# Splitting two pieces of the query weights before the key pieces are taken, and squaring the values after the first query piece's scaling

## The reference

```python
q = x @ Wq + x @ q_A @ q_B          # 16 heads of 64
k = x @ Wk + x @ k_A @ k_B          # 4 heads
v = x @ Wv + x @ v_A @ v_B          # 4 heads
q = _rms_norm(q); k = _rms_norm(k)
q = _apply_rope(q, cos, sin); k = _apply_rope(k, cos, sin)
q = q * q_gain
...                                 # causal softmax attention, y
norm = jnp.sqrt(jnp.sum(v_bt * v_bt, axis=-1, keepdims=True))
vn = v_bt / jnp.maximum(norm, 1e-12)
proj = jnp.sum(y_g * vn, axis=-1, keepdims=True) * vn
out = (y_g - proj) @ Wproj + (y_g - proj) @ p_A @ p_B
```

## Time and profile before

| | before |
|---|---|
| time, three executions | 1453.94, 1456.71, 1459.86 us; median 1456.71 us |
| the profiled execution | 1463.41 us, its span 1461.8 us |
| PE busy | 1416.0 us, 97% of the span |
| DVE, ACT, POOL busy | 844.9 us (58%), 529.3 us (36%), 203.7 us (14%) |
| mean granted clock of TensorE | 0.988 of full speed |

### The profile page before, as it was taken

The page is one execution under the profiler, slowest core; times in us unless marked ns, Lnnn a source line. Parts: engine busy times, 40 slices in busy tenths (PEclk is TensorE's granted clock), DMA queues, the critical chain, the costliest instruction groups (busy, mean ns, idle before and its releaser), DMA issues. The chain is left out here.

```text
span 1461.8 us, 18196 instructions
## 1 busy us (share of the span) xinstructions
PE 1416.0 (97%) x6676; PEld 1156.6 (79%) x6676; DVE 844.9 (58%) x1232; ACT 529.3 (36%) x947; POOL 203.7 (14%) x264
## 2 busy tenths in 40 slices
PE   7999999999999999999999999799998999998998
PEld 6888788888888888888888888676777888877786
DVE  5564455555454545555454556578765576765655
ACT  3222322322233222322223212565432436665561
POOL 3000100000000000000000000555211022122132
PEclk9999999999999999999999999999999899999999
DMA  7353643333333333333333322201100566876766
GB/s 255 144 201 116 264 161 112 116 108 114 130 109 114 108 123 121 115 108 109 134 108 114 110 94 87 87 1 59 34 1 1 179 224 234 287 270 213 269 224 216
DMA packets 43486, 203.64 MB, mean 139 GB/s; under 512 B 5232, under 2 KB 5296, under 8 KB 31984
## 3 DMA queue, kind: packets, MB, share of 16 engines
q1 hardware_dynamic: 30016, 152.32, 29.8%
q0 software_dynamic: 9568, 36.35, 7.8%
q10 hardware_dynamic: 3840, 14.16, 2.4%
HBM read 182.36 MB, written 20.45 MB: 139 GB/s over the span
## 5 line engine op out<-in xcount | busy, mean ns | idle before, releaser
L32 PE MATMUL banks<-V_hi,b_PT_hi 128*128 128x512 f32 x512 | 205.6, 401 | 0.0
L32 PE MATMUL banks<-K_hi,QT_hi 128*128 128x512 f32 x512 | 199.9, 390 | 2.5 <-PEq L157 2.5
L34 PE MATMUL banks<-V_hi,b_PT_lo 128*128 128x512 f32 x512 | 200.2, 391 | 0.0
L1024 ACT ACTIVATE b_PT_hi<-banks 128x512 fp32r<-128x512 f32 x64 | 38.4, 599 | 446.5 <-PE banks L757 446.5
L34 PE MATMUL banks<-K_hi,QT_lo 128*128 128x512 f32 x512 | 200.0, 391 | 0.0
L33 PE MATMUL banks<-K_lo,QT_hi 128*128 128x512 f32 x512 | 199.9, 390 | 0.0
L33 PE MATMUL banks<-V_lo,b_PT_hi 128*128 128x512 f32 x512 | 199.6, 390 | 0.0
L1249 DVE TENSOR_TENSOR b_scores<-banks,b_scores 128x512 f32<-128x512 f32 x64 | 44.2, 691 | 203.4 <-PE banks L34 203.4
L642 POOL DMA_DIRECT2D b_scores<-mask x60 | 32.3, 539 | 640.8 <-PE banks L757 622.9
L2183 DVE TENSOR_TENSOR e_lo<-e_raw,e_hi 128x1024 fp32r<-128x1024 f32 x80 | 94.8, 1230 | 42.0 <-ACT e_hi L2019 40.9
L32 PEld LDWEIGHTS banks<-K_hi,QT_hi 128*128 128x128 f32 x512 | 96.5, 189 | 22.9 <-issue 2.9
(11 more groups left out here) (327 smaller groups left out, 2764.9 us busy)
## 6 DMA issues: line engine op xcount, KB each, us to landing
raw<-kv SPq DMA_DIRECT2D x60, 1024.0 KB, 4.7
e_raw<-w_up SPq DMA_DIRECT2D x40, 512.0 KB, 5.3
e_raw<-w_down SPq DMA_DIRECT2D x40, 512.0 KB, 6.1
b_scores<-mask POOLq DMA_DIRECT2D x64, 256.0 KB, 2.9
d_s_raw<-shared_w SPq DMA_DIRECT2D x32, 512.0 KB, 5.0
raw<-xattn_w SPq DMA_DIRECT2D x11, 1024.0 KB, 4.8
y_dram<-c_zeros ACTq DMA_DIRECT2D x1, 6656.0 KB, 28.1
raw<-attn_w SPq DMA_DIRECT2D x6, 1024.0 KB, 4.7
```

The costliest lines, as they stand in the source:

```text
L32: pe.matmul(out, lhs_hi, rhs_hi, start=first, stop=False)
L34: return pe.matmul(out, lhs_lo, rhs_hi, start=False, stop=last)
L1024: act.activation(PT_hi[:, u % 2, :], T_ps[:, u % 2, :], ACT.Copy).then_inc(b["pt_hi"], 1)
```

## The change

ACT now rounds weights w = 3 ahead of the copy of the low rank products, w = 4 right behind that copy and ahead of take_piece(0), and w = 5 behind take_piece(0) instead of behind take_piece(3). DVE takes the remainder of w = 3 ahead of `lr_s`, and those of w = 4 and w = 5 ahead of the first turn_by_cos. The values' squares stand behind turn_by_cos(4) instead of ahead of it. PE's, POOL's and SP's programs are as they were, and no operation is added or removed. The new file is seven lines shorter, so a line of DVE's part has a number lower by 2 in it up to L1437, and by 1 or more behind it.

```diff
                 weights_hi(2)
+                weights_hi(3)
                 act.wait_ge(s["lr_ready"], 1)
                 act.wait_ge(b["pv_ready"], STEPS)
                 act.activation(lr_hi[:, :], bank[:, 6, :], ACT.Copy).then_inc(s["lr_hi"], 1)
-                weights_hi(3)
+                weights_hi(4)
                 take_piece(0)
-                take_piece(1)
-                weights_hi(4)
-                take_piece(2)
-                take_piece(3)
                 weights_hi(5)
-                take_piece(4)
+                for i in range(1, 5):
+                    take_piece(i)
                 take_piece(5)
...
                 dve.tensor_scalar(gain[:, :], gain[:, :], float(HD) ** -0.5, None, ALU.mult).then_inc(s["gained"], 1)
+                weights_lo(3)
                 dve.wait_ge(s["lr_hi"], 1)
                 dve.wait_ge(b["y_cleared"], 16)
                 dve.scalar_tensor_tensor(lr_s[:, :], f32(lr_hi[:, :]), stack_mask[:, 0:1], bank[:, 6, :],
                                          ALU.mult, ALU.add).then_inc(s["lr_lo"], 1)
                 dve.tensor_tensor(lr_lo[:, :], bank[:, 6, :], f32(lr_hi[:, :]), ALU.subtract).then_inc(s["lr_lo"], 1)
-                weights_lo(3)
                 dve.wait_ge(s["gained"], 1)
+                weights_lo(4)
+                weights_lo(5)
                 turn_by_cos(0)
-                turn_by_cos(1)
-                rotate(0)
-                weights_lo(4)
-                turn_by_cos(2)
-                rotate(1)
-                turn_by_cos(3)
-                rotate(2)
-                weights_lo(5)
-                rotate(3)
+                for i in range(1, 5):
+                    turn_by_cos(i)
+                    rotate(i - 1)
                 unit_values()
-                turn_by_cos(4)
                 rotate(4)
```

## The result

The changed kernel takes 1452.46 us (median of 20 runs, 1449.02 to 1456.09), the kernel before 1457.40 (20 runs): a ratio of 0.9966, interval 0.9956 to 0.9977, which is 4.9 us less (3.4 to 6.4). The forecast was 6.2 less, 1450.5 for a median of 1456.7, with a range of 1446 to 1454.5.

A forecast was written before the change was run, and what follows sets the result against it. TensorE, busy 97%, bounds the kernel. Waits of 2.81 and 4.53, slow clock 2.1 and restarts 0.5 put it 10.0 us ahead; the chain leaves 7.8, then 6.2: 1456.7 - 6.2 = 1450.5 us, range 1446 to 1454.5.

The forecast's parts named there:

- the five cases: Whole kernel: 1449.0 to 1452.0 (0.48), 1447 (0.28), 1452.5 (0.14), 1451.9 (0.06), slower, up to 1464 (0.04).
- the third rival: PE's new waits from 938 to 951 us cost clock: one slow stretch, about 2 us, giving 1452.5; chance 0.14.
- The splits are in time: Remainders come before PE wants them, w = 4 by 2.3 us and w = 5 by 1.65; w = 3 costs nothing.
- The chain up to root(4): POOL, held until DVE's remainder ends at 924.6, goes through roots and sines without pause; root(4) ends at 934.25.
- From root(4) to the last rotation: DVE after 934.25: sums done at 938.95, rotation of piece 4 at 939.7; PE's turn_piece(4) waits 1.7 us.
- Granted clock 1.00 from 925 to 938: Sign expected in the changed profile: full clock in that stretch, around PE's piece 5 and first turnings.
- with the longer one the slow clock behind it: PE's piece 5: removing the 4.53 us wait also removes the slow clock behind it, worth 2.1 us.
- a fall between 938 and 960 us: Sign that the prediction is wrong: the granted clock falls in this stretch, from the last turnings into the heads.
- The sum: Whole kernel: 6.2 us kept at step 2's transposes; 1463.4 becomes 1457.2, or 1450.5 from the median 1456.7.
- POOL's power and root(5): Together 4.9 us, from 939.0 to 944.0; DVE waits for that root in step 0, cutting 7.8 us to 6.2.
- The sums' move is worth 0: DVE: moving the values' squares gives 0, being ahead of the last rotation and POOL's power either way.
- The rival that took the rule literally for the power: POOL's power holds DVE's rotation of piece 4, leaving 4.8 us, so 1451.9; chance 0.06.

The follow-up runs named there:

- e6: Changed kernel with w = 5 back at its old place (copy behind take_piece(3), remainder behind rotate(2)), w = 3 and w = 4 still early; ratio to before 1.0003.
- e3: Changed kernel with 10 discarded matmuls ahead of turn_piece(4) and 3 behind it, filling PE's waits; ratio to before 1.0003.
- e10: Changed kernel with 8 discarded matmuls ahead of turn_piece(4) and none behind it; ratio to before 0.9983.
- e0: The changed kernel run again, nothing altered, as the measure for runs beside it; ratio to before 0.9973.
- e5: Changed kernel with only POOL's order changed: root(5) ahead of the power of the values' sums; ratio to before 0.9976.
- e1: Changed kernel with the values' squares and sums put back ahead of turn_by_cos(4); ratio to before 0.9974.
- e2: Kernel before with only turn_by_cos(4) moved ahead of rotate(3) and the values' squares and sums; ratio to before 1.0000.
- e4: Changed kernel with the values' sums behind the last rotation on DVE, and root(5) ahead of the sums' power on POOL; ratio to before 0.9956.
- e7: Changed kernel with rotate(3) ahead of turn_by_cos(4) instead of behind it; ratio to before 0.9975.
- e4_again: The e4 kernel run again, as the measure for e9 on the same chip; ratio to before 0.9946.
- e9: e4 with POOL's power of the values' sums behind root(6) and DVE's values' unit rows in step 2 behind turn_by_cos(6); ratio to before 0.9955.

## Why the prediction was right, and where its steps were off

- **The number.** 1452.46 us lies in the range, but four of the five cases put their times there, so that says little. It lies outside the forecast's own 1449.0 to 1452.0 and at the third rival's 1452.5, to which the prediction gave 0.14. The gain came from the cause that was named; how much of it would be kept was taken too high, 6.2 for 4.9 us.
- **The splits are in time**: right in each place. The load of w = 3 landed as computed, the copies of w = 4 and w = 5 began within 0.1 us of the forecast behind the four products, and turn_piece(0) came 10.0 us ahead. e6 shows that all of it hangs on w = 5.
- **The chain up to root(4)**: right to 0.2 us, with POOL held by the remainder.
- **From root(4) to the last rotation**: this is the term that was mis-sized. The step read "the scaling and cosines of piece 4 take 1.6 us, a rotation 0.7 to 0.8", from rows in which no sine had begun ahead of them; behind sines they took 1.6 us longer, of which 0.2 was made good by the chain ahead, and the last rotation ended at 24.28 instead of 22.97. I had counted POOL held by DVE, and not DVE held by POOL. The wait was 2.42 us instead of 1.7. The trace before had shown it: a key piece's scaling takes 0.42 us with no sine beside it and 0.67 behind one, in the very stretch of which the prediction noted only that POOL's rows had their plain length. Rows of DVE, DVE and POOL, before:

```profile
920.50 0.42 DVE L1304 TENSOR_TENSOR c_key_piece<-c_key_piece,c_ms 128x256 f32<-128x256 f32 x1 [4.29 <-POOL c_ms L654]
...
929.86 0.67 DVE L1304 TENSOR_TENSOR c_key_piece<-c_key_piece,c_ms 128x256 f32<-128x256 f32 x1 [0.56 <-POOL c_ms L654]
...
929.80 1.05 POOL L663 TENSOR_TENSOR c_sq<-c_key_piece,c_sin 128x128 f32<-128x128 f32 x2
```

- **"Granted clock 1.00 from 925 to 938"**: right, and not enough. The step "with the longer one the slow clock behind it" goes took 2.1 us of gain as kept. The clock fell again behind the new wait. That was the third rival, and it is what happened. The prediction had named a fall between 938 and 960 us as a sign that it was wrong, and this sign came.
- **The sum.** The forecast had step 2 at 34.1 behind the four products; it came at 36.4. e3 and e10, with full clock there, have it at 35.4. So of the 2.3 us missing, 0.9 are the clock; the 1.4 left over fit the 1.3 by which the last rotation was late, which is a subtraction and was not run by itself. It then carried through: 3.9 us at step 2, 3.9 (e0) at SP's load of the shared weights, 4.9 (3.4 to 6.4) and 3.9 (2.3 to 5.7) in the two measured times.
- **POOL's power and root(5)**: sized rightly (5.0 us from the sums), but they were not the limit, as e5 shows: behind the slow clock PE was late as well, and DVE waited 1.28 us for the second scores. With the clock full, in e3, DVE waits 1.60 us for that root; whether it is the limit there was not run.
- **The sums' move is worth 0**: right by e1 and e2. What I passed over is that the sums stood in the chain on either side of turn_by_cos(4): behind the last rotation (e4) they are out of it.
- **The skill's rule.** The Trainium skill (SBUF — State Buffer, SBUF: two separate sides) has whichever of the two starts first hold the port pair for its whole instruction. Here the sines at 934.13 held rotate(3), 1.83 us instead of 0.75, which agrees. POOL's powers hold no product of DVE's that begins inside them, which does not agree: 0.76 us for the rotation at 940.89 of the earlier trace rows, inside the power of the earlier trace rows, and in the changed kernel 0.77 for the last rotation, of which only the first instruction began ahead of the power. The rival that took the rule literally for the power was wrong, and the rule taken for the sines would have pointed at the held rotation.

## What to carry to other kernels

When a wait of the limiting engine is taken away, add up the chain that it covered, engine by engine, up to the next thing the limiting engine needs: here 6.1 of 10.0 us went back that way. In such a chain, look for work whose result is wanted later than its place (the values' sums), and take it out before polishing anything else. And a clock that recovers where a wait goes is only kept if the next wait does not take it again: it was lost at once behind the 2.42 us of the changed kernel, and kept in e4, where that wait was 0.30.

## What the runs showed of the hardware

- Low clock and length of a wait do not go one by one. The clock fell behind waits of 2.42, 3.06 (e7), 3.96 (e1) and 4.94 us. Behind the same 2.81 us it stayed up in the earlier trace rows and fell in e2. It stayed up behind 1.61 us in e4 and 1.83 in e10, but fell behind 1.84 in e3.
- DVE's products of two operands and POOL's sines lengthen each other (1.83 for 0.75, 1.76 for 1.21, 2.91 for 1.93); POOL's powers do not lengthen a product of DVE's that begins inside them (0.76 us at 940.89; so too for 65 such products between 910 and 1000 us in the profiles of before, the changed kernel, e1, e4_again, e5 and e9, none over 0.04 us above its plain length), but a power that begins inside a product of DVE's is lengthened itself (2.93 us in the earlier trace rows, 2.48 for 1.63 in e5).
- Two profiles of kernels 4.9 us apart differed by 11.7 us, 8.8 of it in the mean granted clock (0.988 and 0.994). Places within a trace, counted from a common row, repeated to 0.01 us.
